# The GpSimd bias add in a fused attention and expert block, without its wait for the attention output

## The chip, the cores and the metric

The kernel runs on one core of one Trainium2 chip. The metric is the device time of one execution in microseconds (us). The engines have their own instruction streams: TensorE (PE in the profile), VectorE (DVE), ScalarE (ACT), GpSimd (POOL) and SyncE (SP), which here only issues DMA transfers. They order their work by semaphores: an instruction that is done raises a count, and another engine waits until it has reached a value.

## What is computed

`x` has 2 rows of 2048 tokens with 256 channels. A layer norm with a modulation goes into causal linear attention with 16 heads and 128 exponential features per head, and its projection is added to `x` through the gate `ga`. A second modulated layer norm feeds 4 experts (a shared 256 to 1024 to 256 network with low-rank additions, the top two of four weighted by a router), which are added through `gb`.

```python
h = _layernorm(x, axis=-1) * (1 + ca) + sa
x = x + ga * _L0_attn_ref(h, ...)      # ... y @ W_proj + b_proj at its end
h = _layernorm(x, axis=-1) * (1 + cb) + sb
x = x + gb * _L0_ffn_ref(h, ...)
```

The step that the change touches is the bias part of the second line: `x + ga * b_proj`, before the matrix product `ga * (y @ W_proj)` is added.

## The kernel before

The tokens are worked off in 8 blocks of 512 (`NB` = 8, `T` = 512; four token tiles of 128, `NT` = 4). Each engine has a loop over the first 7 blocks and then the last block written out. Within a block PE, DVE and ACT run `attend` (the attention of block n, with the front of block n+1 woven in) and `after_attend` (projection, residual, second layer norm, experts). `attend` treats the 16 heads in four groups (`gr` = 0 to 3). Per group PE forms scores (L511), products of values and features (L526), transposes the state parts (L535), reads the running state (L545) and transposes the output (L552). The order on every engine is the order of the code; nothing is scheduled elsewhere.

On DVE one group is: copy half of the products out of PSUM (L1123); a causal mask (L1079); `advance_state`, which copies the running state into `s_sb` (L1091, an SBUF to SBUF copy of 128x128 float32) and then adds four state parts from PSUM one after the other (L1095, four instructions, the last into `state`); two more causal masks (L1079); `add_reads` (L1099), for whose result PE's output transpose L552 waits; the division (L1106, L1108, L1110), which writes `y`. PE's state reads for tiles 0 and 1 wait for the copy and two of the adds, those for tiles 2 and 3 for all four. `y_step` counts the three instructions of each division, so that `3 * GROUPS` is the end of the last group's division. In groups 0 and 1 DVE also takes the statistics of the next block's first layer norm (L1020 to L1006, in group 0) and applies them (L1011, in group 1).

POOL does little. Per block it copies the gate rows of this block into `mod2_now` (L1363, raises `mod2_set`), computes `rstd` and `shift` of the next block's first layer norm (L1354, L1357, after DVE's L1006), adds `bpg_now` (the gated projection bias, a part of `mod2_now`) to `xr`, the four token tiles of `x` (L1372, 128x1024 float32 in place, raises `xr_biased`), and computes `rstd` and `shift` of the second layer norm. At the end of a loop step it waits for `scaled`, the four products of the gate and the expert output (L1247), before it may overwrite `mod2_now`.

DVE's `residual` (L1156) waits for `xr_biased` and for the projection of PE (L617), and adds the projection to `xr`. At the block's end DVE's `finish` adds `xr` to the expert output `tg` (L1252, two instructions per block, 128x512 each, both inputs in SBUF). SP then stores the output and loads `xr` for the next block (L365), and `tok` for the one after the front (L362).

Of the kernel before, what the change touches and what calls it, by code (L numbers as in the profile page):

```python
# [50 lines left out]
GROUPS = H // GROUP  # L51
# [46 lines left out]
def wait(eng, signal, n, c):  # L98
    eng.wait_ge(signal.sem, signal.at(n, c))


def build(nc, x, w_attn, b_attn, w_proj, b_proj, omega, wg, bg, wi, wo, lora_a, lora_b, cond, wmod,
          consts, norm_rows, out, parts_out, norms_out):
    ctx = ExitStack()
    with ctx:
# [3 lines left out]
        def sig(name, per=0):  # L109
            return Signal(ctx.enter_context(nc.semaphore(name)), per)  # L110
# [137 lines left out]
        oT_added, o_ps, y_step = sig("oT_added", GROUPS), sig("o_ps", GROUPS), sig("y_step", 3 * GROUPS)  # L248
# [24 lines left out]
        def over_tiles(row, k):  # L273

            return row.rearrange("p (o w) -> p o w", o=1).broadcast_to([P, k, row.shape[1]])
# [1035 lines left out]
        @block.gpsimd  # L1311
        def _(pool):
            def setup():
                pool.memset(low_raw, 0.0).then_inc(set_pool.sem, 1)
                pool.memset(mk1[:], 0.0).then_inc(set_pool.sem, 1)
                pool.memset(mk2[:], 0.0).then_inc(set_pool.sem, 1)

            def setup_lora():
                pool.wait_ge(ld_lora.sem, 16)
                pool.wait_ge(set_pool.sem, 3)  # L1320
                for half, mk in enumerate((mk1, mk2)):
                    for q in range(3):
                        pool.tensor_copy(mk[:, :, 32 * q:32 * q + LORA].rearrange("p t (e r) -> p t e r", r=R),
                                         lora_raw[:, LORA_TILES * half:LORA_TILES * (half + 1)])\
                            .then_inc(set_pool.sem, 1)

            def gate(q, rows):

                pool.wait_ge(gates_sb.sem, q + 1)
                pool.tensor_scalar(half_sign, rows, 0.0, 0.5, ALU.is_ge, ALU.subtract).then_inc(set_gate.sem, 1)  # L1330
                pool.wait_ge(set_gate.sem, 4 * q + 1)
                pool.tensor_tensor(rows, rows, half_sign, ALU.mult).then_inc(set_gate.sem, 1)
                pool.wait_ge(set_gate.sem, 4 * q + 2)
                pool.tensor_scalar(rows, rows, 0.125, 4.0, ALU.max, ALU.mult).then_inc(set_gate.sem, 1)
                pool.wait_ge(set_gate.sem, 4 * q + 3)
                pool.tensor_tensor(rows, rows, half_sign, ALU.mult).then_inc(set_gate.sem, 1)
                pool.wait_ge(set_gate.sem, 4 * q + 4)

            def gate_bias():

                pool.wait_ge(ld_wp.sem, 16 * 3)
                pool.tensor_tensor(mod2[:, :, C:2 * C], ga_rows, over_tiles(bp_row, B), ALU.mult)\
                    .then_inc(bias_gated.sem, 1)
                pool.wait_ge(bias_gated.sem, 1)

            def gate_projection():
                for row in range(B):
                    pool.tensor_tensor(wp_ga[:, row], wp, over_tiles(ga_rows[:, row], KT),
                                       ALU.mult).then_inc(wp_done.sem, 1)

            def rstd_of(n, vec, sem):

                wait(pool, vec, n, 2 * NT + 1)
                pool.tensor_tensor(rstd[:], var_eps[:], neg_half[:], ALU.pow).then_inc(sem.sem, 1)  # L1354
                wait(pool, vec, n, 2 * NT + 2)
                wait(pool, sem, n, 1)
                pool.tensor_tensor(shift[:], neg_mean[:], rstd[:], ALU.mult).then_inc(sem.sem, 1)  # L1357

            def attend(n, front_next):
                row = n // BLOCKS_PER_ROW  # L1360
                src = mod2[:, row, 0:2 * C] if isinstance(n, int) else \
                    mod2[:, bass.ds(row, 1), 0:2 * C].rearrange("p o c -> p (o c)")
                pool.tensor_copy(mod2_now[:], src).then_inc(mod2_set.sem, 1)  # L1363
                if front_next:
                    rstd_of(n + 1, ln1_vec, ln1_pool)

            def residual(n):
                wait(pool, xr_loaded, n, 16)
                wait(pool, mod2_set, n, 1)
                wait(pool, y_step, n, 3 * GROUPS)  # L1370
                two = xr[:]
                pool.tensor_tensor(two, two, over_tiles(bpg_now, NT), ALU.add).then_inc(xr_biased.sem, 1)  # L1372

            setup()
            pool.wait_ge(set_const.sem, 1)
            rstd_of(0, ln1_vec, ln1_pool)
            setup_lora()
            gate(0, ga_rows)
            gate_bias()
            gate(1, gb_rows)  # L1380
            gate_projection()
            pool.wait_ge(set_mod.sem, 4)
            with pool.Fori(0, NB - 1) as i:
                attend(i, True)
                residual(i)
                rstd_of(i, ln2_vec, ln2_pool)
                wait(pool, scaled, i + 1, NT)
            attend(NB - 1, False)
            residual(NB - 1)
            rstd_of(NB - 1, ln2_vec, ln2_pool)  # L1390

# [45 lines left out]
```

## Time and profile before

| | us |
|---|---|
| median of 3 runs | 812.75 |
| the runs | 809.42, 812.75, 813.11 |
| the profiled execution | 809.42 |
| its span, first to last instruction | 807.2 |
| time outside the span | 2.2 |
| mean granted TensorE clock in it, share of full speed | 0.989 |

The profile is of one execution. Times in it are counted from the start of the span. A block of the loop takes 93.5 us: POOL's L1372 starts at 100.72, 194.22 and 287.72 us in the first three. The second block's attention begins at about 148 us and its residual at 198 us; that block is shown below as the example, and the block before and those after repeat it to within some hundredths of a us. A timeline row that gathers several instructions (x2, x32) gives the time from the start of the first to the end of the last.

### The profile page before, as it was taken

How to read it: one execution, taken by the hardware profiler on the slowest of the kernel's cores; microseconds unless marked ns; L12 is line 12 of the kernel's file. 1: busy time of each engine (PE TensorE's matmuls, PEld its weight loads, DVE VectorE, ACT ScalarE, POOL GpSimd, SP SyncE). 2: the span in 40 equal slices, each digit the busy share in tenths (PEclk: the TensorE clock that was granted, in tenths of full speed). 3: DMA queues.
4: the chain of work that ended last, by engine and by line, in shares of the span. 5: the costliest groups of instructions: out<-in, count | busy, mean ns of one | idle time of the engine just before them, and what ended most of it. 6: DMA issues, size and time to landing. Idle time of an engine off the chain costs nothing.

```text
span 807.2 us, 16965 instructions
## 1 busy us (share of the span) xinstructions
PE 755.9 (94%) x6138; PEld 603.7 (75%) x6138; DVE 531.3 (66%) x1276; ACT 413.5 (51%) x764; POOL 62.5 (8%) x72
## 2 busy tenths in 40 slices
PE   3989999999999999999999999999999999999596
PEld 3768768887698767887688876987679776887366
DVE  4346676776767676776766767776767767665456
ACT  3475535564456454664365545565446644664232
POOL 1170010001000010001000010000100010000100
PEclk9989999999999999999999999999999999999999
DMA  7850073202802064201722037020742018110000
GB/s 259 228 150 1 28 188 81 78 0 85 205 2 78 0 177 116 69 9 41 201 50 78 0 107 185 0 78 0 203 90 78 0 52 215 25 54 2 0 1 27
DMA packets 42867, 65.35 MB, mean 81 GB/s; under 512 B 5064, under 2 KB 19168, under 8 KB 42720
## 3 DMA queue, kind: packets, MB, share of 16 engines
q1 hardware_dynamic: 42848, 65.09, 30.0%
q8 instruction: 13, 0.21, 0.1%
q14 instruction: 6, 0.05, 0.0%
HBM read 39.91 MB, written 25.17 MB: 81 GB/s over the span
## 4 chain that ended last, share of the span: by engine, by line
PE 84%; DVE 9%; ACT 2%; issue 2%; SPq 1%; POOL 1%; DMA 1%; DVEq 0%; ACTq 0%
PE pa L511 13%; PE prod L526 7%; PE ring L490 6%; PE ring L375 5%; PE pa L375 5%; PE pa L377 4%; PE pa L376 4%; PE ring L376 4%; PE ring L377 4%; PE prod L545 4%; PE pa L617 4%; PE ring L495 4%; PE ring L645 2%; PE prod L511 2%; PE ring L698 2%; PE prod L535 2%
## 5 line engine op out<-in xcount | busy, mean ns | idle before, releaser
L511 PE MATMUL pa<-phq,phkT 128*128 128x128 f32 x896 | 115.1, 276 | 0.0
L511 PEld LDWEIGHTS pa<-phq,phkT 128*128 128x128 f32 x896 | 107.9, 191 | 2.4 <-issue 1.6
L837 ACT ACTIVATE phq<-ring 128x512 f32<-128x512 f32 x96 | 60.0, 625 | 84.8 <-PE ring L490 83.8
L1079 DVE TENSOR_TENSOR am_phk<-pa,const 128x512 f32<-128x512 f32 x112 | 74.2, 685 | 33.1 <-PE pa L511 33.1
L1232 DVE SCALAR_TENSOR_TENSOR am_phk<-ring,am_phk 128x512 f32<-128x512 f32 x64 | 44.2, 691 | 53.1 <-PE ring L698 53.1
L901 ACT ACTIVATE qk_r<-phq 128x512 fp32r<-128x512 f32 x64 | 40.5, 632 | 63.7 <-DVE phq L1241 63.7
L375 PE MATMUL pa<-wo_r,qk_r 128*128 128x256 f32 x256 | 72.1, 282 | 0.6 <-DVE qk_l L1237 0.6
L377 PE MATMUL pa<-wo_l,qk_r 128*128 128x256 f32 x256 | 72.1, 282 | 0.0
L376 PE MATMUL pa<-wo_r,qk_l 128*128 128x256 f32 x256 | 71.8, 281 | 0.0
L526 PE MATMUL prod<-am_phk,v_ones 128*32 128x256 f32 x1024 | 61.9, 382 | 4.6 <-DVE tg L1110 4.6
L837 ACT ACTIVATE phkT<-ring 128x512 f32<-128x512 f32 x98 | 61.9, 632 | 0.0
L375 PE MATMUL ring<-h_r,wi_r 128*128 128x512 f32 x128 | 57.7, 451 | 4.2 <-DVE am_phk L1232 3.6
L490 PE MATMUL ring<-xq,omega_x 100*128 100x512 f32 x194 | 60.5, 431 | 0.0
L837 ACT ACTIVATE am_phk<-ring 128x512 f32<-128x512 f32 x97 | 53.7, 617 | 10.7 <-PE ring L495 10.6
L886 ACT ACTIVATE phq<-ring 128x512 f32<-128x512 f32 x64 | 37.5, 586 | 32.7 <-PE ring L686 32.7
L526 PEld LDWEIGHTS prod<-am_phk,v_ones 128*32 128x32 f32 x1024 | 31.3, 109 | 28.5 <-DVE am_phk L1079 6.0
L376 PE MATMUL ring<-h_r,wi_l 128*128 128x512 f32 x128 | 50.7, 396 | 0.0
L377 PE MATMUL ring<-h_l,wi_r 128*128 128x512 f32 x128 | 50.6, 395 | 0.0
L375 PEld LDWEIGHTS pa<-wo_r,qk_r 128*128 128x128 f32 x256 | 48.3, 189 | 2.6 <-DVE qk_l L1237 1.0
L376 PEld LDWEIGHTS pa<-wo_r,qk_l 128*128 128x128 f32 x256 | 48.4, 189 | 1.5
L377 PEld LDWEIGHTS pa<-wo_l,qk_r 128*128 128x128 f32 x256 | 48.1, 188 | 0.0
L1237 DVE TENSOR_TENSOR qk_l<-phq,qk_r 128x512 fp32r<-128x512 f32 x64 | 43.8, 684 | 5.9 <-ACT qk_r L901 5.6
(204 smaller groups left out, 1560.3 us busy)
## 6 DMA issues: line engine op xcount, KB each, us to landing
xq<-qk_parts SPq DMA_DIRECT2D x48, 512.0 KB
qk_parts<-qk_r SPq DMA_DIRECT2D x32, 256.0 KB, 4.0
qk_parts<-qk_l SPq DMA_DIRECT2D x32, 256.0 KB, 4.4
tok<-in_L_attn_x SPq DMA_DIRECT2D x8, 512.0 KB, 4.7
xr<-in_L_attn_x SPq DMA_DIRECT2D x8, 512.0 KB, 4.0
out_x<-tg SPq DMA_DIRECT2D x16, 256.0 KB, 2.3
norm_parts<-norm_r SPq DMA_DIRECT2D x16, 128.0 KB, 2.5
norm_parts<-norm_l SPq DMA_DIRECT2D x16, 128.0 KB, 3.0
```

The costliest lines, as they stand in the source:

```text
L375: pe.matmul(dst, w_r, v_r, start=first, stop=False, skip_group_check=shared)
L376: pe.matmul(dst, w_l, v_r, start=False, stop=False, skip_group_check=shared)
L377: return pe.matmul(dst, w_r, v_l, start=False, stop=last, skip_group_check=shared)
L490: mm = pe.matmul(dst[:], omega_x[:, k // 2 * M:(k // 2 + 1) * M], xq[:, p // HALF, k % 2, p % HALF, :], start=True, stop=True)
L511: mm = pe.matmul(score_bank(q, a)[:, tt], phkT[:, q % 2, a, tt], phq[:, q // 2 % 2, 2 * (q % 2) + a, tt], start=True, stop=True)
L526: mm = pe.matmul(prod[j * VA:(j + 1) * VA, c], v_ones[:, c, GROUP * gr + j, :], both, start=True, stop=True)
L837: act.activation(dst, src, ACT.Exp).then_inc(exp_done.sem, 1)
L886: act.activation(g[:, f % 4, :], z_bank[f % 4][:], ACT.Relu).then_inc(r1_done.sem, 1)
L901: act.activation(g_r[:, k % 3, :], g[:, k % 4, :], ACT.Copy).then_inc(g_high.sem, 1)
L1079: dve.tensor_tensor(am[:, 2 * (q % 2) + a, :].rearrange("p (c t) -> p c t", c=NT), score_bank(q, a)[:].rearrange("p (c t) -> p c t", c=NT) ...
L1232: dve.scalar_tensor_tensor(r2[:, f % 2, :], z_bank[f % 4][:], 0.0, rho, ALU.max, ALU.mult).then_inc(r2_done.sem, 1)
L1237: dve.tensor_tensor(g_l[:, k % 3, :], g[:, k % 4, :], g_r[:, k % 3, :].bitcast(F32), ALU.subtract).then_inc(g_low.sem, 1)
```

## The change

One wait is removed on POOL, in `residual`: the one for the end of the last group's division. What stays ahead of the add are the waits for the load of `xr` and for `mod2_set`. The instructions of all engines and their order stay as they are.

```diff
--- before.py
+++ after.py
@@ -1367,7 +1367,6 @@
             def residual(n):
                 wait(pool, xr_loaded, n, 16)
                 wait(pool, mod2_set, n, 1)
-                wait(pool, y_step, n, 3 * GROUPS)
                 two = xr[:]
                 pool.tensor_tensor(two, two, over_tiles(bpg_now, NT), ALU.add).then_inc(xr_biased.sem, 1)
```

## Rows read from the trace of the kernel before

**Rows 1.** The page, the chain of work that ended last: shares of the span.

```profile
PE 84%; DVE 9%; ACT 2%; issue 2%; SPq 1%; POOL 1%; DMA 1%; DVEq 0%; ACTq 0%
```

**Rows 2.** Timeline, POOL, second block: start us, us, engine, line, what, [idle before <-releaser].

```profile
149.87 0.61 POOL L1363 COPY mod_now<-mod 128x512 f32 x1 [39.67 <-DVE tg L1247]
166.26 1.01 POOL L1354 TENSOR_TENSOR rstd<-var_eps,neg_half 128x4 f32<-128x4 f32 x1 [15.78 <-DVE neg_mean L1006]
167.34 0.20 POOL L1357 TENSOR_TENSOR shift<-neg_mean,rstd 128x4 f32<-128x4 f32 x1
194.22 2.36 POOL L1372 TENSOR_TENSOR xr<-xr,mod_now 128x1024 f32<-128x1024 f32 x1 [26.68 <-DVE tg L1110]
```

**Rows 3.** One line's instructions, L1372: duration in ns min/median/max.

```profile
L1372 POOL TENSOR_TENSOR xr<-xr,mod_now x8: 2347/2361/2363, 100.7 to 753.4; 128x1024 f32<-128x1024 f32 x8
```

**Rows 4.** Timeline, DVE, same columns, around the residual of the second block.

```profile
198.23 0.69 DVE L1156 TENSOR_TENSOR xr<-pa,xr 128x512 f32<-128x512 f32 x1 [0.61 <-PE pa L617]
```

**Rows 5.** Timeline, DVE, same columns, group 1 of the second block.

```profile
167.81 0.69 DVE L1079 TENSOR_TENSOR am_phk<-pa,const 128x512 f32<-128x512 f32 x1 [0.85 <-PE pa L511]
168.42 0.22 DVE L1091 COPY s_sb<-state 128x128 f32 x1
168.67 0.93 DVE L1095 TENSOR_TENSOR s_sb<-s_sb,prod 128x128 f32<-128x128 f32 x3
169.63 0.29 DVE L1095 TENSOR_TENSOR state<-s_sb,prod 128x128 f32<-128x128 f32 x1
169.84 1.28 DVE L1079 TENSOR_TENSOR am_phk<-pa,const 128x512 f32<-128x512 f32 x2
171.07 0.69 DVE L1099 TENSOR_TENSOR s_sb<-prod_sb,prod 128x512 f32<-128x512 f32 x1
```

**Rows 6.** Timeline, PE, same columns, the same stretch.

```profile
169.92 1.08 PE L545 MATMUL prod<-phq,s_sb 128*32 128x128 f32 x32
170.94 1.20 PE L490 MATMUL ring<-xq,omega_x 100*128 100x512 f32 x4
171.97 0.60 PE L552 MATMUL prod<-const,s_sb 128*128 128x128 f32 x4
```

**Rows 7.** Timeline, DVE, same columns, end of the first block.

```profile
148.14 1.26 DVE L1247 SCALAR_TENSOR_TENSOR tg<-pa,w,mod_now 128x256 f32<-128x256 f32 x3
149.32 1.71 DVE L1252 TENSOR_TENSOR tg<-tg,xr 128x512 f32<-128x512 f32 x2
```

**Rows 8.** One line's instructions, L1252, in 148 to 152 us: ns min/median/max.

```profile
L1252 DVE TENSOR_TENSOR tg<-tg,xr x2: 681/895/1109, 149.3 to 149.9; 128x512 f32<-128x512 f32 x2
```

**Rows 9.** Groups by line and shape, DVE: count | busy us, mean ns.

```profile
L1123 DVE COPY prod_sb<-prod 128x512 f32<-128x512 f32 x32 | 22.1, 692 | 35.6 <-PE prod L526 35.5
...
L1091 DVE COPY s_sb<-state 128x128 f32 x28 | 6.2, 222 | 5.8 <-PE prod L535 5.8
...
L1212 DVE COPY am_phk<-exo 128x512 f32<-128x512 f32 x8 | 3.4, 419 | 0.0
```

**Rows 10.** One line's instructions, L1041, in 193 to 204 us: ns min/median/max.

```profile
L1041 DVE SCALAR_TENSOR_TENSOR qk_l<-ring,qk_bias,qk_r x2: 741/742/743, 194.7 to 202.3; 128x512 fp32r<-128x512 f32 x2
L1041 DVE SCALAR_TENSOR_TENSOR qk_l<-pa,qk_bias,qk_r x1: 741/741/741, 194.1 to 194.1; 128x512 fp32r<-128x512 f32 x1
```

**Rows 11.** The chain of waits, 166.2 to 176 us: start us, us, what.

```profile
172.13 0.44 PE prod L552 x4
```

**Rows 12.** Last block: loads of xr (us to landing), and the copy of the state.

```profile
L365 SPq DMA_DIRECT2D xr<-in_L_attn_x x7: 418/418/421, 151.7 to 712.6; - x7
...
DMA to landing us min/median/max: 3.7/4.2/4.7
...
718.58 0.22 DVE L1091 COPY s_sb<-state 128x128 f32<-128x128 f32 x1
```

## The prediction

> **What bounds the kernel now.** I read the page's chain of work that ended last first, then the timeline of POOL, since the edit is on POOL's stream, and then the timelines of DVE and PE at the place the add leaves and at the place it goes to. The chain is 84% PE, 9% DVE and 1% POOL [rows 1]: PE's order of work sets the time, and another engine matters where PE has to wait for it. So the question is not how long POOL works, but whether anyone's wait for POOL, or anything that POOL disturbs, ends last on PE's path.
>
> **The wait that goes.** In the second block POOL's add starts at 194.22 us, after 26.68 us of idling for the division L1110, and takes 2.36 us, to 196.58 [rows 2]; the eight of them take 2347 to 2363 ns [rows 3]. The only one who needs it is DVE's residual L1156, which starts at 198.23 and was released by PE's projection L617, not by POOL [rows 4]. That is 1.65 us after the add had ended. Having the biased `xr` sooner therefore buys nothing: 0 us, and what is late there is the projection. Nor is POOL itself needed for something between: its next instruction is the `rstd` of the second norm, which waits for DVE behind the residual. The add has no neighbour at its old place that it slows: of the two L1041 on DVE that start at 194.1 and 194.7, while it runs, and the one at 202.3, the shortest takes 741 ns and the longest 743 [rows 10]. So leaving that place gains 0 too.
>
> **Where the add goes.** With the wait gone, the stream runs from the `shift` of the next block's first norm, L1357, straight into the add. In the second block L1357 is over at 167.34 + 0.20 = 167.54. The pair L1354, L1357 has 0.07 us between the end of one and the start of the other (166.26 + 1.01 = 167.27, then 167.34) [rows 2], and I take the same here: the add runs from 167.61 to 169.97. Its other two waits don't hold it: `xr` for this block was loaded long before (loads land 3.7 to 4.7 us after their issue, the first of the loop being issued at 151.7 [rows 12]), and `mod2_now` was written at 149.87 [rows 2]. The same holds in the blocks before and after, as a block repeats every 93.5 us.
>
> **What stands beside it there.** DVE is in group 1: a mask L1079 at 167.81, the copy of the running state L1091 at 168.42 (0.22 us), the four adds L1095 at 168.67 to 169.92, two masks, and `add_reads` L1099 at 171.07, over at 171.76 [rows 5]. PE reads the state at 169.92 and transposes the output, for which it needs L1099, at 171.97 [rows 6]. So DVE is 171.97 - 171.76 = 0.21 us ahead of PE at L1099; the chain of waits, which counts L552 from the end of what was before it, puts it at 172.13 [rows 11], which makes the margin 0.37. A delay of DVE in this chain costs PE all but that much, because from L1091 to L1099 DVE has no gap: 168.64 to 168.67, and each after that starts as the one before ends [rows 5].
>
> **Does the add delay DVE?** The trace has one place where a POOL instruction of size stands beside DVE instructions with both inputs in SBUF: the block's end. L1247, for which POOL's copy L1363 waits, is over at 149.40 [rows 7], yet the copy starts only at 149.87 and ends at 150.48 [rows 2]. The first L1252 runs from 149.32 and takes 681 ns; the second starts at 149.9 and takes 1109 [rows 8]. The two together end at 149.32 + 1.71 = 151.03 [rows 7], 0.55 us after POOL's copy. So each waits for the other's instruction: the copy for the first L1252, the second L1252 for the end of the copy, and what it then still needs is 0.55 of its 0.68 us, 0.13 less than all. DVE instructions with an operand in PSUM show nothing of it [rows 10].
>
> L1091 has one input, in SBUF, and its output in SBUF. Such copies run at about double rate here: 512 elements take 419 ns from SBUF (L1212) and 692 ns from PSUM (L1123), and L1091 takes 222 for 128 [rows 9]. It draws more from SBUF per unit of time than one stream does, as L1252 does, and that makes me put it on L1252's side and not on L1041's. No row shows such a copy beside POOL, so its price is bounded: from below 0, if only instructions with two inputs are held; not below 0, since no one is released earlier by POOL [rows 4]. From above by a hold to the end of the add: L1091 would end 0.22 - 0.13 = 0.09 us after 169.97, at 170.06, in place of 168.64, a delay of 1.42 us. Less the margin of 0.21 to 0.37 this is 1.05 to 1.21 us of PE's time per block. I take the full hold, at 1.15 us, because L1252 was held to the very end of POOL's instruction.
>
> The Trainium skill, page "SBUF — State Buffer", section "Who interferes with whom", says that VectorE's second read and write ports to SBUF are GpSimd's only ones, that the pair is locked for a whole instruction, and that copies in a two-port mode and instructions with two SBUF inputs contend for it, whoever is first. By that rule L1091 is held and the cost is that of the full hold; without it, it would be 0. The L1252 rows (681 and 1109 ns) agree for two inputs; for a copy no row here shows it. Its page "VectorE: DVE Perf Modes", section "Mode 2×_2P", gives float32 copies within SBUF that mode, which agrees with 419 against 692 ns. The rule speaks against this change.
>
> **How far the delay travels.** The four L1095 move by the same 1.42 us: the second ends at about 169.28 + 1.42 = 170.70 and the fourth at 169.92 + 1.42 = 171.34, so PE's state reads, which began at 169.92, first wait 0.8 us. They end about 0.5 us after the fourth add, at 171.9 in place of 170.94. L490 then takes its 1.03 us to 172.9, while DVE does the two masks and L1099, now over at 171.76 + 1.42 = 173.18. L552 starts at 173.2 in place of 171.97. The waits overlap, so they are not added up: the last one decides, 1.2 us by this count. Everything behind L552 on PE, DVE and ACT hangs on PE's order and moves with it; no load or fixed clock stands later in the block that could swallow it (DMA has 1% of the chain [rows 1]).
>
> **The sum.** Seven blocks have this meeting: 7 x 1.15 = 8.05 us. In the last block there is no next front, and POOL comes to the add as soon as `xr` is there: the load is issued at 712.6 and lands 3.7 to 4.7 us later, at 716.3 to 717.3, and the add ends at 718.7 to 719.7; L1091 is due at 718.58 [rows 12]. By the same working that is a delay of 0 to 1.0 and a cost of 0 to 0.8; I take 0.2. Together +8.2 us. Against the profiled execution, 809.42 us (807.2 of span and 2.2 around it), this gives 817.7. That execution was the fastest of three, and the median is 3.3 higher: 812.75 + 8.2 = 821.0, which I predict for the median.
>
> **Rivals.** *Copies are not held.* If only a second input meets POOL, nothing in 167.6 to 170.0 does, as L1079 and L1095 take one of their inputs from PSUM. The time stays: 812.75 (809.4 to 813.1), not slower. For it: the trace only shows two-input instructions held. Against it: the doubled rate of L1212. It decides at the margin: a delay of L1091 under 0.21 us costs nothing.
> *POOL lets go between parts.* The add might hold SBUF for pieces of its 2.36 us. With a delay of half, 0.7 us, the cost is 0.7 - 0.3 = 0.4 per block, 2.8 in all: 815.6. Against it: L1363 held on to its end, though it is 0.61 long and of another kind.
> *The masks are held too.* Then L1079 of 167.81 would wait to 169.97 and L1091 would start 0.6 later, at 170.6: a delay of 2.1, less 0.3, is 1.8 per block, 12.6 in all: 825.5. Against it: L1041, also with one SBUF tensor, ran unharmed under the add [rows 10].
> *Faster.* It needs a wait for `xr_biased` that ended last, and there is none [rows 4]: 811 or less only by chance.
>
> **How the numbers follow.** The forecast has 0.70, copies not held 0.14, pieces 0.09, masks too 0.05, faster 0.02. The forecast's own range is the base of 809.4 to 813.1 plus 7.4 to 9.3, 817 to 822.5. The range for 8 in 10 takes in the pieces too: 815.5 to 823.5. A measurement of this kernel can tell about 0.5% from no change, 4 us. The forecast and the masks lie above it, and of the pieces about half: slower 0.79, same 0.19, faster 0.02.
>
> **What would show it.** In the trace after: POOL's add at 167.6 in the second block, unchanged at 2.36 us; one L1091 per block at about 1.65 us in place of 0.22 (or started late by as much), the other three at 0.22; PE waiting on DVE at L545 (0.8 us) and at L552; L1156 still released by L617; a block of about 94.6 us in place of 93.5. The prediction is wrong if all L1091 stay at 0.22 us, or if the block grows less than DVE's delay minus 0.4 us, which would mean slack further down that I have not found.

## The result

| | before | changed |
|---|---|---|
| median of 6 runs, us | 812.68 | 819.22 |
| the runs | 809.08 to 813.11 | 816.56 to 820.12 |
| profiled execution, us | 809.42 | 816.52 |
| its span, us | 807.2 | 814.1 |
| period of a block, us | 93.48 | 94.44 |

The changed kernel is slower: ratio 1.0085, 95% interval 1.006 to 1.0108. The period is taken from the starts of POOL's first `rstd` (L1354) in the second and the seventh block, a fifth of the distance: (633.67 - 166.26) / 5 before and (639.46 - 167.26) / 5 after. It comes from one profiled execution of each kernel and lies between 93.47 and 93.49 us in all seven kernels of this document that lose next to nothing, while the executions of the kernel before lie more than 4 us apart, so the experiments are read by it. Seven times 0.96 us is 6.7 of the 6.9 us that the span has grown.

The page of the changed kernel has more of DVE in its chain, where [rows 1] has 84% PE and 9% DVE:

```profile
PE 82%; DVE 11%; ACT 2%; issue 2%; SPq 1%; POOL 1%; DMA 1%; DVEq 0%; ACTq 0%
```

The timeline of POOL, in the second block, shows the add straight behind L1357 (start us, us, engine, line, what). The add is L1371 here, since one line above it is gone:

```profile
167.26 1.01 POOL L1354 TENSOR_TENSOR rstd<-var_eps,neg_half 128x4 f32<-128x4 f32 x1 [15.78 <-DVE neg_mean L1006]
168.34 0.20 POOL L1357 TENSOR_TENSOR shift<-neg_mean,rstd 128x4 f32<-128x4 f32 x1
168.50 2.36 POOL L1371 TENSOR_TENSOR xr<-xr,mod_now 128x1024 f32<-128x1024 f32 x1
204.35 1.02 POOL L1354 TENSOR_TENSOR rstd<-var_eps,neg_half 128x4 f32<-128x4 f32 x1 [33.49 <-DVE neg_mean L1006]
```

This block is 1.0 us late as a whole, against [rows 2], because the block before it has already paid. The timeline of DVE beside it, to be held against [rows 5]:

```profile
168.79 0.69 DVE L1079 TENSOR_TENSOR am_phk<-pa,const 128x512 f32<-128x512 f32 x1 [0.84 <-PE pa L511]
169.40 1.54 DVE L1091 COPY s_sb<-state 128x128 f32 x1
170.97 0.93 DVE L1095 TENSOR_TENSOR s_sb<-s_sb,prod 128x128 f32<-128x128 f32 x3
171.94 0.29 DVE L1095 TENSOR_TENSOR state<-s_sb,prod 128x128 f32<-128x128 f32 x1
172.14 1.28 DVE L1079 TENSOR_TENSOR am_phk<-pa,const 128x512 f32<-128x512 f32 x2
173.34 0.67 DVE L1099 TENSOR_TENSOR s_sb<-prod_sb,prod 128x512 f32<-128x512 f32 x1
```

The mask at 168.79 is unchanged though it runs under the add. The copy of the state, L1091, takes 1.54 us in place of 0.22 and ends at 170.94, the add at 170.86. The adds, masks and L1099 behind it have their old lengths to within 0.02 us and are simply late. The timeline of PE in the same stretch, against [rows 6]:

```profile
171.64 1.29 PE L545 MATMUL prod<-phq,s_sb 128*32 128x128 f32 x32 [0.66 <-DVE s_sb L1095]
172.85 1.20 PE L490 MATMUL ring<-xq,omega_x 100*128 100x512 f32 x4
174.07 0.66 PE L552 MATMUL prod<-const,s_sb 128*128 128x128 f32 x4
...
176.96 1.94 PE L526 MATMUL prod<-am_phk,v_ones 128*32 128x256 f32 x32
```

PE now waits 0.66 us for L1095 ahead of its state reads, and L552 starts at 174.07, 0.06 us after L1099 is done. The chain of waits of this stretch goes over DVE, where before it was PE alone:

```profile
169.40 1.55 DVE s_sb L1091
...
170.97 0.30 DVE s_sb L1095
...
171.30 0.30 DVE s_sb L1095
...
171.64 1.29 PE prod L545 x32
```

How often this happens can be worked out from the busy time of the 28 instances of L1091 that the loop has (count | busy us, mean ns): it was 6.2 us before [rows 9] and is 15.4 now. The difference, 9.2, is seven times the 1.32 us by which the copy above is longer, so one copy per block is held. The second line has all 32 with the last block's (ns min/median/max), and the last block is in the timelines of POOL and DVE:

```profile
L1091 DVE COPY s_sb<-state 128x128 f32 x28 | 15.4, 551 | 5.8 <-PE prod L535 5.8
```

```profile
L1091 DVE COPY s_sb<-state x32: 215/227/1562, 64.1 to 755.3; 128x128 f32 x28, 128x128 f32<-128x128 f32 x4
```

```profile
723.34 2.37 POOL L1371 TENSOR_TENSOR xr<-xr,mod_now 128x1024 f32<-128x1024 f32 x1 [5.21 <-DMA xr<-in_L_attn_x]
```

```profile
725.34 0.45 DVE L1091 COPY s_sb<-state 128x128 f32<-128x128 f32 x1
```

There the add had to wait for `xr` and was nearly over when the copy came: 0.45 us. PE lost nothing: from the seventh block's first `rstd` to the last L1354 of the program it is 128.39 us (639.46 to 767.85) in place of 127.43 (633.67 to 761.10), and that 0.96 is the seventh block's own. Finally the residual, which in [rows 4] waited for the projection and not for POOL:

```profile
200.18 0.69 DVE L1156 TENSOR_TENSOR xr<-pa,xr 128x512 f32<-128x512 f32 x1 [0.61 <-PE pa L617]
```

It still waits for PE's L617, by the same 0.61 us. The early `xr` has no taker.

### The profile page after: what moved, and what is told of

It reads as the page before. It is cut to its first block, busy times and chain, and to the rows that moved or that the text cites. A ratio compares the mean times of both kernels' runs of the same rounds, so it can differ in the third digit from the quotient of the medians.

```text
span 814.1 us, 16958 instructions
## 1 busy us (share of the span) xinstructions
PE 758.6 (93%) x6138; PEld 603.5 (74%) x6138; DVE 540.2 (66%) x1276; ACT 413.8 (51%) x764; POOL 62.2 (8%) x72
## 4 chain that ended last, share of the span: by engine, by line
PE 82%; DVE 11%; ACT 2%; issue 2%; SPq 1%; POOL 1%; DMA 1%; DVEq 0%; ACTq 0%
PE pa L511 11%; PE prod L526 7%; PE ring L490 6%; PE ring L375 5%; PE pa L375 5%; PE pa L377 4%; PE pa L376 4%; PE prod L545 4%; PE ring L376 4%; PE ring L377 4%; PE pa L617 4%; PE ring L495 3%; PE ring L645 2%; PE prod L511 2%; PE ring L698 2%
## 5 line engine op out<-in xcount | busy, mean ns | idle before, releaser
L1079 DVE TENSOR_TENSOR am_phk<-pa,const 128x512 f32<-128x512 f32 x112 | 74.2, 685 | 32.8 <-PE pa L511 32.8
L526 PE MATMUL prod<-am_phk,v_ones 128*32 128x256 f32 x1024 | 61.9, 382 | 4.6 <-DVE tg L1110 4.6
L490 PE MATMUL ring<-xq,omega_x 100*128 100x512 f32 x194 | 60.0, 429 | 0.0
L526 PEld LDWEIGHTS prod<-am_phk,v_ones 128*32 128x32 f32 x1024 | 31.4, 110 | 28.8 <-DVE am_phk L1079 6.3
```

Of the source, the lines that this page charges most:

```text
L490: mm = pe.matmul(dst[:], omega_x[:, k // 2 * M:(k // 2 + 1) * M], xq[:, p // HALF, k % 2, p % HALF, :], start=True, stop=True)
L526: mm = pe.matmul(prod[j * VA:(j + 1) * VA, c], v_ones[:, c, GROUP * gr + j, :], both, start=True, stop=True)
L1079: dve.tensor_tensor(am[:, 2 * (q % 2) + a, :].rearrange("p (c t) -> p c t", c=NT), score_bank(q, a)[:].rearrange("p (c t) -> p c t", c=NT) ...
```

## Experiments

One theory stood against three rivals. **The hold**: while POOL's add runs, a DVE instruction that needs a second path to SBUF (two streams at once) is held to the end of POOL's instruction, and the whole cost comes from that one copy's lateness. **Rivals**: any DVE instruction from SBUF to SBUF is held; the hold isn't per instruction; or an early add costs something else as well.

**Another place for the add.** The changed kernel, with a wait that lets the add begin after group 1's state adds:

```diff
                 wait(pool, mod2_set, n, 1)
+                wait(pool, s_step, n, 2 * (NT + 1))
                 two = xr[:]
```

> The changed kernel with one more wait on POOL: the add waits for s_step of group 1 (the four adds L1095 done, about 169.9 us in the second block), so it runs from 169.9 to 172.3 beside masks and L1099, which take one input from PSUM. Theory (only the meeting with L1091 costs): all L1091 at 0.22 us, ratio to before 0.998 to 1.002. Rival (an early add costs something wherever it stands in the attention, by slowing DVE or ACT in general): ratio 1.005 to 1.010 with L1091 at 0.22 us and another group of DVE longer.

Measured: ratio 1.0006 (0.9985 to 1.0027), period 93.47 us. The add (timeline of POOL) and the line of L1091:

```profile
169.35 2.39 POOL L1372 TENSOR_TENSOR xr<-xr,mod_now 128x1024 f32<-128x1024 f32 x1 [2.45 <-DVE state L1095]
```

```profile
L1091 DVE COPY s_sb<-state x32: 216/218/229, 63.4 to 747.8; 128x128 f32 x28, 128x128 f32<-128x128 f32 x4
```

An add that is 24 us earlier than in the kernel before costs nothing if it doesn't meet L1091. That rules out a general price of an early add as far as this other place can show it; the run with the lateness and without POOL, below, tests it for the place of the change.

**The copy out of the add's way.** The changed kernel with its add where it is, and each group's copy of the state moved ahead of L1123:

```diff
                 for gr in range(GROUPS):
...
+                    advance_state(n, gr, True)
                     wait(dve, prod_ps, n, 2 * gr + 2)
```

With `True`, `advance_state` does the copy alone; the call at its old place is left with the adds.

> The changed kernel, with each group's copy of the state (L1091) moved on DVE from behind the wait for PE's transposes to ahead of the copy of the products (L1123), where it has no one to wait for. In group 1 of the second block it runs at about 167.2, over before the add begins at 168.5. Theory: the copy is 0.22 us everywhere, nothing is left that the add can hold, and DVE's chain from L535 to L1099 is 0.22 us shorter in all groups; PE waited for it in group 3 (L545 2.8 us, L552 4.6 us in all), so the time is that of before or up to 3 us less: ratio to before 0.996 to 1.000. Rival (the cost of the early add isn't its meeting with L1091): ratio 1.006 to 1.009.

Measured: ratio 0.9987 (0.997 to 1.0005), period 93.49 us. The copy (timeline of DVE) is over before the add (timeline of POOL; its line number has moved) begins:

```profile
165.83 0.22 DVE L1091 COPY s_sb<-state 128x128 f32 x1
```

```profile
167.18 2.37 POOL L1374 TENSOR_TENSOR xr<-xr,mod_now 128x1024 f32<-128x1024 f32 x1
```

So the meeting of these two instructions is the cost, seen from either side. The hoped-for gain in group 3 is not there: the period is that of before.

**Half an add at a time.**

```diff
-                two = xr[:]
-                pool.tensor_tensor(two, two, over_tiles(bpg_now, NT), ALU.add).then_inc(xr_biased.sem, 1)
+                for b in range(2):
+                    two = xr[:, 2 * b:2 * b + 2]
+                    mm = pool.tensor_tensor(two, two, over_tiles(bpg_now, 2), ALU.add)
+                mm.then_inc(xr_biased.sem, 1)
```

> The changed kernel with the add as two instructions of 128x512 in place of one of 128x1024, 1.27 us each by L1348. Theory (POOL holds for one whole instruction and lets DVE in between two): the first half runs from 168.5 to 169.75 in the second block, where L1091 is due at 169.4, so L1091 takes 0.35 + 0.10 = 0.45 us, a delay of 0.25 to 0.35, of which 0.2 is hidden: 0 to 0.15 us per block, ratio to before 1.000 to 1.002; the second half starts late, behind the copy. Rival (POOL keeps its hold from one instruction to the next, or the hold goes by the work queued): L1091 at 1.5 us again and a ratio of 1.008.

Measured: ratio 1.002 (0.9999 to 1.0041), period 93.49 us. Timelines of POOL and DVE:

```profile
166.83 2.50 POOL L1372 TENSOR_TENSOR xr<-xr,mod_now 128x512 f32<-128x512 f32 x2
```

```profile
168.07 1.27 POOL L1372 TENSOR_TENSOR xr<-xr,mod_now 128x512 f32<-128x512 f32 x1
```

```profile
167.74 0.45 DVE L1091 COPY s_sb<-state 128x128 f32 x1
```

The second POOL row is the second half by itself. The copy takes 0.45 us, as expected, and ends at 168.19, 0.09 us after the first half (166.83 + 1.27) and 1.14 before the end of the second. So the hold is per instruction. That the second half would start late, behind the copy, is not what the rows show: it starts at 168.07, while the copy is still on record, and the pair takes no longer than two halves. The lateness of 0.23 us costs 0.01 us per block, so PE has at least that much in hand. The interval of the ratio alone would not have told that from a small loss.

**Which copies are held.** The first attempt wrote the copy as a multiplication by two columns of ones:

```diff
-                dve.tensor_copy(s_sb[:, 0, :], start).then_inc(s_step.sem, 1)
+                one = v_ones[:, 0, 0, DH:DH + 1]
+                dve.tensor_scalar(s_sb[:, 0, :], start, one, one, ALU.mult, ALU.mult).then_inc(s_step.sem, 1)
```

> The changed kernel, with the copy of the state (L1091) written as a tensor_scalar by two per-partition columns of ones, the form of L1011, which takes 407 ns for 256 elements and so runs at single rate; the same values, some 0.29 us in place of 0.22. Theory (POOL's add holds back the double-rate copy by its second path to SBUF): the four L1091 of a block all take 0.28 to 0.30 us, the add still begins at 168.5 in the second block, and the time is that of before, 812.7, +0.07 us per group at most, so a ratio to before of 1.000 to 1.003. Rival (any DVE instruction that reads and writes SBUF is held by POOL): one L1091 per block at 1.6 us and a ratio of 1.008 as in the changed kernel.

Measured: ratio 1.0088 (1.0053 to 1.0123), period 94.45 us; this instruction's line, and for comparison L1011 in the kernel before (ns min/median/max):

```profile
L1092 DVE TENSOR_SCALAR s_sb<-state,v_ones x32: 336/346/1556, 64.6 to 755.9; 128x128 f32 x28, 128x128 f32<-128x128 f32 x4
```

```profile
L1011 DVE TENSOR_SCALAR tok<-tok,mv,rstd x32: 403/407/413, 8.9 to 643.0; 128x256 f32<-128x256 f32 x32
```

It was held as before, 1.53 us in the second block. By its number that was the rival's outcome, but the premise was wrong: 128 elements take 336 ns at the shortest (346 in the median) and 256 take 407, so 128 more cost 60 to 70 ns. That is half of the 133 that they cost at the single rate of 1.04 ns per element, which the reductions of the next runs give (128 elements in 0.277 us, 1200 in 1.39). The form has a larger fixed part and runs at double rate too. (That two such columns are also read from SBUF is another difference; this run doesn't separate it.) The test needed a single-rate form:

```diff
-                dve.tensor_copy(s_sb[:, 0, :], start).then_inc(s_step.sem, 1)
+                dve.tensor_reduce(s_sb[:, 0, :], start.rearrange("p (m o) -> p m o", o=1), AX.X,
+                                  ALU.add).then_inc(s_step.sem, 1)
```

> Again the changed kernel with the copy of the state in another form, now as a tensor_reduce over an axis of length one, which gives the same values. The form of the first attempt turned out to cost only 69 ns more for 256 elements (L1011, 405) than for 128 (336), so it ran at double rate too and told nothing apart. Here the sizes of the trace point to single rate: about 0.29 us expected, 128 elements at the 1.04 ns each of the DVE adds. Theory (POOL's add holds DVE instructions that draw at double rate or have two SBUF inputs, through a second path): none of the four per block is held, all at 0.27 to 0.31 us, block period 93.5 us, ratio to before 0.999 to 1.003. Rival (every DVE instruction from SBUF to SBUF is held): one per block at 1.55 us, block period 94.5, ratio 1.008.

Measured: ratio 1.0002 (0.9981 to 1.0023), period 93.48 us. Timelines of POOL and DVE, and the line:

```profile
168.03 2.36 POOL L1372 TENSOR_TENSOR xr<-xr,mod_now 128x1024 f32<-128x1024 f32 x1
```

```profile
168.93 0.27 DVE L1091 TENSOR_REDUCE s_sb<-state 128x128 f32 x1
```

```profile
L1091 DVE TENSOR_REDUCE s_sb<-state x32: 274/277/290, 64.6 to 749.0; 128x128 f32 x28, 128x128 f32<-128x128 f32 x4
```

Same input, same output, same moment, in the middle of the add, and not held: 0.27 us. So an instruction from SBUF to SBUF is not held as such. What the copy has and the reduction lacks is the double rate (the copies of [rows 9] grow by 0.51 ns per element from 128 to 512, the reductions by 1.04 from 128 to 1200), and with it, by the theory, the second path. The two held forms and the free one agree with that; other differences between the forms were not taken apart, and the path itself is argued, not seen.

**The same lateness without POOL.** The kernel before, with its add in the old place, and one unused reduction ahead of the copy in group 1:

```diff
+                if gr == 1:
+                    weights = wi_r[:].rearrange("p k f -> p (k f)").bitcast(F32)
+                    dve.tensor_reduce(scratch[:, 0:4], weights[:, 0:1200].rearrange("p (t c) -> p t c", t=4),
+                                      AX.X, ALU.add)
                 dve.tensor_copy(s_sb[:, 0, :], start).then_inc(s_step.sem, 1)
```

> The kernel before, POOL's add in its old place, with one unused DVE instruction ahead of the copy of the state in group 1 of each block: a sum over 128x1200 of a constant weight, about 1.25 us. It makes DVE as late there as the add made it (1.30 us), without any add. Theory (the cost is DVE's lateness less what PE has in hand, about 0.2 us at L552 and 0.15 us recovered at the next L490): block period 94.3 to 94.5 us against 93.5, the last block longer by the same, ratio to before 1.008 to 1.010. Rival (the early add costs by something else too, as POOL's traffic beside PE or ACT): the period stays below 94.2 and the ratio below 1.006.

Measured: ratio 1.0071 (1.0046 to 1.0096), period 94.44 us. Timelines of DVE and PE (L552 is L553 here):

```profile
169.15 1.39 DVE L1094 TENSOR_REDUCE scratch<-wi_r 128x4 f32<-128x1200 f32 x1
170.46 0.22 DVE L1096 COPY s_sb<-state 128x128 f32 x1
```

```profile
171.37 1.29 PE L546 MATMUL prod<-phq,s_sb 128*32 128x128 f32 x32 [0.65 <-DVE s_sb L1100]
...
173.81 0.66 PE L553 MATMUL prod<-const,s_sb 128*128 128x128 f32 x4
```

DVE is late by 170.46 - 169.15 = 1.31 us, and the period is that of the changed kernel to the hundredth. Nothing else of the early add is needed to explain it. The ratio came out below the 1.008 that I had put as the lower end, and its interval takes in both that and the rival's 1.006, so it is the period that decides, and it is what was expected.

**The meeting that the kernel before has.** The kernel before, with POOL's gate copy L1363 behind both L1252:

```diff
-                wait(pool, scaled, i + 1, NT)
+                wait(pool, fin, i, 2)
```

> The kernel before, with POOL waiting at the end of a block for fin (the two L1252 done) in place of scaled, before it copies the gate rows (L1363): the one meeting that the kernel before has. Theory: the second L1252 takes 0.68 us in place of 1.10, DVE is 0.43 us earlier at the masks of the next block; PE's products L526 there start 0.1 us after the last mask, with PE's own work filling the time before, so little of it shows: 0 to 0.1 us per block, ratio to before 0.998 to 1.001. Rival (that meeting is on the path as well): 0.3 to 0.4 us per block, ratio 0.996 to 0.997.

Measured: ratio 0.9996 (0.9977 to 1.0015), period 93.48 us. The line of L1252, which averages 864 ns in the kernel before, and PE's first products of the third block:

```profile
L1252 DVE TENSOR_TENSOR tg<-tg,xr x16: 678/682/686, 150.3 to 808.2; 128x512 f32<-128x512 f32 x16
```

```profile
246.93 1.18 PE L490 MATMUL ring<-xq,omega_x 100*128 100x512 f32 x4
248.04 1.93 PE L526 MATMUL prod<-am_phk,v_ones 128*32 128x256 f32 x32
```

The same two in the kernel before:

```profile
245.95 1.18 PE L490 MATMUL ring<-xq,omega_x 100*128 100x512 f32 x4
247.05 1.93 PE L526 MATMUL prod<-am_phk,v_ones 128*32 128x256 f32 x32
```

The hold is gone from all L1252 and nothing is gained: PE goes from L490 into L526 in 1.11 us with the gate copy late and in 1.10 without, so it was not waiting for what the hold made late. This meeting was real and off the path.

**Both repairs at once.** The kernel before, with the copies early and the gate copy late:

```diff
+                    advance_state(n, gr, True)
                     wait(dve, prod_ps, n, 2 * gr + 2)
...
-                wait(pool, scaled, i + 1, NT)
+                wait(pool, fin, i, 2)
```

> The kernel before with its wait kept, plus two edits that take DVE's instructions out of POOL's way or off the chain: each group's copy of the state ahead of L1123, and POOL's gate copy behind fin. Theory: with the copies early DVE's margin ahead of PE grows by 0.22 us in each group, which only groups 3 (where PE waits for L1095 and L1099) can use, and the gate copy gives 0 to 0.1 us: 0 to 3 us in all, ratio 0.996 to 1.000. Rival (the margins on DVE are worth nothing anywhere, PE's order alone sets the time): 0.999 to 1.001.

Measured: ratio 0.9996 (0.9978 to 1.0013), period 93.48 us. That is the rival's outcome: these margins gave no gain here, and no version beats the kernel before beyond its uncertainty.

## Why the prediction was right

The forecast was 821.0 us and slower by 8.2; the median is 819.22, slower by 6.5, inside the range of 815.5 to 823.5. Step by step:

- **The wait that goes buys nothing.** Right: L1156 waits for L617 by 0.61 us, before and after.
- **Leaving the old place gains nothing.** Right as far as can be seen: L1041 has the same length, and the run with the add behind the state adds, also away from the old place, is not faster.
- **The add meets L1091.** Right. I had put POOL's start 0.07 us behind L1357; it starts at 168.50, 0.04 before L1357's recorded end of 168.54 (168.34 + 0.20). That is 0.11 us sooner, and the hold ends as much sooner.
- **The copy is held to the end of the add.** Right, and it was the open step: the trace of before showed it for two inputs only. L1091 ends 0.08 us after the add, the double-rate multiplication took 1.53 us in the same place, and the reduction 0.27. The lateness is 1.30 us where I had 1.42: L1091 ends at 170.94, and without the hold it would end 1.0 us after the 168.64 of [rows 5], at 169.64. The Trainium skill's page "SBUF — State Buffer", section "Who interferes with whom", gives the hold for double-rate copies and says that `tensor_reduce` never contends on this chip; the traces agree with both.
- **Each waits for the other at the block's end.** Half right. The second L1252 does wait for POOL's copy. But that POOL's copy L1363 started late because of the first L1252 was misread: in the run with the gate copy behind both L1252 it starts 0.44 us after the instruction that it waits for (L1252, over at 245.10), with only masks beside it, and in the kernel before 0.47 after L1247. So that delay is POOL's own. Only the last block's gate copy, which comes 0.23 us after L1247 (over at 710.30), is held: 0.84 us in place of 0.61. These are its row in the kernel before and one of the run with the gate copy late:

```profile
710.53 0.84 POOL L1363 COPY mod_now<-mod 128x512 f32<-128x512 f32 x1 [39.44 <-DVE tg L1247]
```

```profile
245.54 0.61 POOL L1363 COPY mod_now<-mod 128x512 f32 x1 [40.83 <-DVE tg L1252]
```

The sum didn't use this reading.
- **PE's margin.** Mis-sized. I had 0.21 by the timeline or 0.37 by the chain, and took 1.15 of cost out of 1.05 to 1.21, which is a margin of 0.27. By the timeline L1099 ends 1.25 us late (174.01 against 171.76 + 1.00); less 0.21, and with the 0.06 that L552 now starts behind it, L552 is late by 1.10 us (174.07 against 171.97 + 1.00). But PE then makes up 0.14. Before the change L526 started 3.03 us after L552, at 175.00 (timeline of PE, before, with the weight load, PEld, ahead of it):

```profile
174.57 0.19 PEld L490 LDWEIGHTS ring<-xq,omega_x 100*128 100x128 f32 x1 [0.30 <-ACT am_phk L837]
175.00 1.93 PE L526 MATMUL prod<-am_phk,v_ones 128*32 128x256 f32 x32
```

After it, 176.96 - 174.07 = 2.89. Of the steps between, the second run of L490, whose last weight load had waited 0.30 us for ACT, is the one that got shorter: 1.07 us before and 0.94 after in the chains. The delay at the end of the group is 0.96 us, so 0.34 of the 1.30 is hidden (0.35 in the run without POOL), near the chain's 0.37. So two terms were about a tenth of a us off, both to the same side: the lateness 0.12 too large and the margin 0.07 too small, 1.15 in place of 0.96, seven times. That is 1.3 us of the 1.7 by which the forecast was over. Of the other 0.3, 0.2 is the last block's, and the rest is within what the medians of the two kernels can tell.
- **The last block.** I had 0.2; L1091 was held for 0.23 us there and PE lost nothing.
- **The rivals.** *Copies are not held* and *the masks are held too* fell to the rows of DVE after (1.54 us for L1091, 0.69 for L1079). *POOL lets go between parts* is true between two instructions and false within one.

## What to carry to other kernels

A wait on a lightly used engine can be worth keeping although nobody needs its result late: it also decides whom the instruction behind it meets. Before such an instruction is let loose, list what the neighbours on VectorE do in its new place, and look for those with two inputs in SBUF or at double rate; one of 0.2 us, held for 1.3, in a chain with 0.35 us in hand, cost 0.9% here (ratio 1.0085). If it must be early, split it, move the copy, or give the copy a single-rate form: all three brought the time back.

## What the runs showed of the hardware

**The hold works by instruction and by form.** Under the same POOL instruction a float32 copy of 128x128 from SBUF to SBUF took 1.54 us in place of 0.22, and a reduction over an axis of one element, with the same input and output, 0.27. The reduction is only 0.05 us dearer than the copy when both are free, and it doesn't need to know where POOL is.

**`tensor_scalar` with two columns as scalars is at double rate with a large fixed cost**: 336 to 346 ns for 128 elements and 407 for 256. A mean duration tells the rate only if two sizes of the same form are compared.

**How long TensorE's clock is low in the last block differs between executions, and the whole time goes with it by up to 4 us.** The executions of the kernel before gather around 809 and around 813 us. One execution of each kernel has a trace, so two kernels of the same period are compared: the kernel before (809.42 us), whose row comes first, and the one with the add behind the state adds (812.26 us). The columns are length, busy us of PE, PEld, DVE, ACT and POOL with their counts, clock, DMA share and GB/s:

```profile
740.00:760.00 20.00, 13.66 (x155) 9.94 (x153) 10.87 (x29) 1.68 (x3) 2.35 (x1) 1.00 0.00 1
```

```profile
740.00:760.00 20.00, 14.90 (x143) 10.72 (x143) 8.29 (x21) 1.79 (x3) 0.00 (x0) 0.78 0.00 1
```

Up to 750 us the two are alike: PE is busy for 7.42 of 10 us and granted full speed, 2.4 GHz. From 750 to 760 the first stays there, while the second is granted 0.55 of it, so it is at the lower level, 1.2 GHz, nearly all the time. From 760 to 770 both have a low stretch (0.66 and 0.67). From the last block's gate copy to its second norm that is 50.6 us (710.53 to 761.10) against 54.5 (709.80 to 764.33), in a stretch where PE has gaps because no next front fills them. Of the other traces of this period, the three that stay at full speed up to 760 us are of executions of 808.70 to 810.33 us, and the two that don't are of 810.42 and 813.76. That the clock makes the two groups is likely from this and not shown: the mean clock of the executions doesn't part them (0.987 at 809.12 and at 812.27 us, same kernel). Why one execution drops for longer than another was not tried either. It makes the medians of 6 to 30 runs uncertain by some 0.2%, and the period of the blocks the better witness.
